# Rows of 264 for the second experts, normalised by ScalarE, with the expert chosen in the mixing, a shorter placing chain and mixing in five groups

## The chip, the cores and the metric

The kernel runs on one core of one Trainium2 chip. The metric is the time of one execution on the device in microseconds (us); for one core this is the core's own time from launch to end. Lower is better.

## The reference

A graph of 3125 nodes with 256 features and 50,000 edges goes through two attention layers, each followed by a feed-forward layer of experts. The change lies in the last two of the four parts. They compute, for x with one row per node:

```python
# L1_gnn, after the edges: agg, deg are sums over the edges of a node
msgs = jnp.where(deg[:, None, None] > 0, agg, V)
out = msgs.reshape(N, H * D) @ Wo + bo
x1 = out + node_features
x = x + (x1 - mu) / jnp.sqrt(var + 1e-05) * gamma + beta
# L1_ffn, on the layer norm of x: 32 experts, one per node, hidden size 64
xf = layernorm(x)
idx = jnp.argmax(xf @ router_w.T + router_b, axis=-1)
h = relu(jnp.einsum('nd,ndh->nh', xf, W1[idx]) + b1[idx])
x = x + relu(jnp.einsum('nh,nhd->nd', h, W2[idx]) + b2[idx])
```

## The kernel before

All arithmetic on features is in float32. Nodes are padded to 25 windows (WIN) of 128 rows; a window has one node per partition. Each part of the network is one or more blocks, and at the end of a block all engines meet at a barrier. The last three blocks are what the change touches.

**Mixing** (`mix_second`). The windows go through in groups, GROUPS_OF: five of 4 windows and one of 5. In round r VectorE does: `message(r + 2)` (sum of messages divided by its weight, or the node's own value where it has no edges; `val` is loaded from DRAM for that), the inverse standard deviation of the first norm, `apply_first(r)` (scale, gamma, residual into `k.comb[:, w, 0:D]`), the statistics of the second norm, `add_residual(r + 1)` (the product with Wo from PSUM plus `xin1_rows`, two windows per instruction), the statistics of the first norm of group r + 1, and at last `inverse(1, r)` and `second_shift(r)`. TensorE turns the messages (`turn`), multiplies by Wo (`multiply`, two windows per PSUM bank `ps_y`, three banks in a ring; the wait on `z_done` keeps a bank until `add_residual` has read it), and then, for group r, turns the normalised rows and makes the 32 logits of each node. ScalarE copies from PSUM to SBUF for each of these (`take_messages` in L2481, `xs` in L2507, logits in L2510), takes the square roots of the variances (`deviation`), and writes the normalised rows to `k.comb[:, w, D:2*D]` (L2502). Everything on an engine runs in the order of its code. In particular `deviation(1, r)` stands behind `take_messages(r + 2)` and behind the logits of group r - 1.

SyncE's queue loads `val` and `xin` two groups ahead. Its loop is: wait for `msg` of r, load `val` of r + 2, wait for `shift_ready` of r, load `xin` of r + 2. So the `val` of a group is issued behind the `xin` of the group before. After the loop it issues the weights of the second experts (L2385 to L2391).

**Placing** (`place`). VectorE adds the router's bias, takes the maximum, and makes `hot`, one of 32 for each of 25 x 128 nodes, by six instructions over 800 elements. TensorE multiplies `hot` by a matrix of ones (`ps_c`: nodes per window and expert) and by a triangle (`ps_b`: nodes before this one in its window); VectorE waits for both (`counted`, 2). It copies the counts, makes a running sum over the windows for each expert, rounds each expert's total up to whole tiles of 128, and from these makes each node's slot. GpSimd then scatters the 25 windows of `k.comb` to `sorted_rows` in DRAM, one indirect DMA per window (L2622). A row has COMB = 520 floats: x, the normalised x, and 8 copies of the node's number.

**Experts** (`feed_second`). 56 tiles of 128 sorted rows. For tile t, SyncE loads the tile (L2760) once tile t - 6 has been finished by VectorE (ring `rows`, IN = 6). TensorE's iteration t is: turn the rows of t (L2816), first product of t - 1 (L2827), turn the hidden rows of t - 2 (L2834), second product of t - 3 (L2839). ScalarE copies the turned rows (L2799) and applies the Relu (L2794). VectorE adds b1 (L2782), casts the node's number (L2772), and makes y (L2774). GpSimd scatters y to the output (L2749).

## Time and profile before

| | us |
|---|---|
| median of 3 runs | 1996.17 |
| lowest, highest | 1983.52, 2001.51 |
| the profiled execution | 1986.1 |
| its span, first to last instruction | 1984.4 |
| mixing, from the first instruction to the end of the block | 1699.8 to 1813.4 |
| placing, up to the slots | 1813.4 to 1836.5 |
| the scatter of the sorted rows, up to the next block | 1836.5 to 1874.2 |
| experts | 1874.2 to 1984.4 |

Times in the rows are microseconds from the span's start. The blocks are one after the other, so a block that is shorter moves all behind it. Of the engines, PE is TensorE's multiplying, PEld its loading of weights, DVE VectorE, ACT ScalarE, POOL GpSimd; SPq is SyncE's queue, and a DMA_DIRECT2D there is the issuing, not the transfer. What stands in brackets behind an instruction is the idle time of its engine before it and what ended it.

### The profile page before, as it was taken

The page shows a single profiled execution, that of the slowest core. Times are in us where ns is not written, and L with a number is a line of the kernel's source. Part 1 is how long each engine was busy: PE and PEld are TensorE (multiplying, and loading weights), DVE is VectorE, ACT ScalarE, POOL GpSimd, SP SyncE. Part 2 cuts the span into 40 slices and gives each one's busy share as a digit, 9 for nine tenths or more (in the row PEclk, how much of TensorE's full clock was granted, in tenths as well). Part 3 has the DMA queues.
Part 4 walks back from the last instruction along what each step waited for, and adds up shares of the span by engine and source line. Part 5 has one row for each costly group of instructions (what it writes and reads, how often), then busy time and mean ns, then how long its engine had stood idle before and what let it go on. Part 6 is the DMA issues. An engine that isn't in the chain of part 4 may idle for free. (4 is left out here: it accounts for less than half of the span.)

```text
span 1984.4 us, 29978 instructions
## 1 busy us (share of the span) xinstructions
PE 1396.1 (70%) x7038; PEld 974.9 (49%) x7038; DVE 1466.0 (74%) x3709; ACT 1114.5 (56%) x4299; POOL 1066.4 (54%) x1119
## 2 busy tenths in 40 slices
PE   5447656756666669998857787788877877674176
PEld 4334444444444457775534455555555554353154
DVE  5568778878878843366869999999999998776143
ACT  2247666676666643232533888888888887122033
POOL 2377777777776000003247777777777775100555
PEclk9667777777777759999977989988898888865599
DMA  5744444444443028001467767666777763225465
GB/s 123 196 128 125 138 124 125 125 136 125 124 137 85 1 75 299 1 1 48 159 213 232 203 199 207 200 197 200 200 202 203 201 199 123 64 65 120 167 197 138
DMA packets 141117, 287.90 MB, mean 145 GB/s; under 512 B 25507, under 2 KB 66977, under 8 KB 140821
## 3 DMA queue, kind: packets, MB, share of 16 engines
q0 software_dynamic: 58192, 175.85, 31.0%
q1 hardware_dynamic: 82758, 110.13, 18.9%
q8 instruction: 67, 1.10, 0.2%
q14 instruction: 100, 0.82, 0.1%
HBM read 241.17 MB, written 48.86 MB: 146 GB/s over the span
## 5 line engine op out<-in xcount | busy, mean ns | idle before, releaser
L773 POOL DMA_INDIRECT e_rows<-h_rows,src_col x416 | 433.0, 1041 | 127.0 <-issue 125.2
L1226 POOL DMA_INDIRECT e_rows<-kv_rows,src_col x320 | 309.0, 966 | 98.1 <-issue 60.6
L942 ACT ACTIVATE e_rows<-e_rows 128x32 f32<-128x32 f32 x1664 | 357.7, 305 | 0.8
L1011 PE MATMUL e_sum<-e_rows,e_of_dst 128*128 128x264 f32 x832 | 290.2, 501 | 77.8 <-DVE e_rows L870 71.3
L1481 ACT ACTIVATE e_rows<-e_rows 128x64 f32<-128x64 f32 x1168 | 292.8, 335 | 0.3
L1559 PE MATMUL e_query<-q,e_to_dst 128*128 x1248 | 215.4, 309 | 91.2 <-DVE e_rows L1294 70.5
L1011 PEld LDWEIGHTS e_sum<-e_rows,e_of_dst 128*128 128x128 f32 x832 | 194.0, 249 | 128.1 <-DVE e_rows L870 78.5
L1600 PE MATMUL e_sum<-e_rows,e_of_dst 128*128 128x260 f32 x640 | 202.9, 443 | 3.3 <-DVE acc L1382 2.9
L1559 PEld LDWEIGHTS e_query<-q,e_to_dst 128*128 128x128 bf16 x1248 | 124.6, 104 | 148.1 <-issue 105.9
L1382 DVE TENSOR_TENSOR acc<-acc,e_sum 128x260 f32 x299 | 125.7, 420 | 51.5 <-PE e_sum L1600 21.7
L1600 PEld LDWEIGHTS e_sum<-e_rows,e_of_dst 128*128 128x128 f32 x640 | 120.7, 212 | 30.9 <-DVE acc L1382 12.5
L2154 POOL TENSOR_TENSOR xb<-acc,bo 128x1280 f32<-128x1280 f32 x3 | 7.4, 2468 | 193.9 <-DMA beta<-in_L_gnn_beta 193.9
L1226 POOL DMA_INDIRECT x<-kv_rows,src_col x96 | 92.3, 961 | 33.8 <-issue 19.0
L1287 DVE TENSOR_TENSOR e_rows<-e_rows,e_relation 128x512 f32<-128x512 f32 x160 | 108.5, 678 | 1.4 <-DMA e_rows<-kv_rows,src_col 1.4
L1294 DVE TENSOR_TENSOR e_rows<-e_rows,e_query 128x512 f32<-128x512 f32 x160 | 108.0, 675 | 0.0
L1300 DVE TENSOR_REDUCE e_scores<-e_rows 128x8 f32<-128x512 f32 x160 | 107.7, 673 | 0.0
L880 DVE TENSOR_TENSOR acc<-acc,e_sum 128x264 f32 x208 | 86.7, 417 | 27.8 <-DVE e_bwd L799 14.0
L1552 PEld LDWEIGHTS e_relation<-rel,e_to_typ 64*128 64x128 bf16 x1248 | 52.7, 100 | 103.8 <-issue 71.5
L986 PE MATMUL e_turned<-ident,e_scores 128*128 128x128 f32 x26 | 12.1, 463 | 129.7 <-DVE e_scores L794 129.7
L1552 PE MATMUL e_relation<-rel,e_to_typ 64*128 64x64 bf16 x1248 | 78.2, 201 | 30.1 <-DVE e_to_dst L1278 12.7
L947 ACT ACTIVATE e_factor<-e_fall 8x1 f32<-8x1 f32 x26 | 5.3, 202 | 162.9 <-DVE e_fall L820 162.9
L1239 POOL TENSOR_TENSOR acc<-acc,e_taken 128x260 f32 x114 | 86.6, 760 | 18.6 <-DVE acc L1382 8.5
(420 smaller groups left out, 2993.4 us busy)
## 6 DMA issues: line engine op xcount, KB each, us to landing
sorted_rows<-zeros SPq DMA_DIRECT2D x1, 14560.0 KB
rows<-sorted_rows SPq DMA_DIRECT2D x56, 260.0 KB, 3.0
e_rel<-step_rel SPq DMA_DIRECT2D x26, 512.0 KB, 4.0
e_to_dst<-step_rel SPq DMA_DIRECT2D x52, 256.0 KB, 4.0
e_rows<-h_rows,src_col POOLq DMA_INDIRECT x416
e_to_typ<-step_typ SPq DMA_DIRECT2D x52, 128.0 KB
e_rows<-kv_rows,src_col POOLq DMA_INDIRECT x320, 3.7
kv_rows<-kv SPq DMA_DIRECT2D x5, 768.0 KB, 3.5
```

Of the source, the lines that this page charges most:

```text
L773: pool.indirect_dma_start(out=g[t // BATCH % R][:, t % BATCH, :], out_offset=None, in_=k.h_rows[:, :], in_offset=bass.IndirectOffsetOnAxis ...
L942: ins = act.activation(x, x, ACT.Copy, scale=row[:, D + h:D + h + 1])
L1011: pe.matmul(psm[t % NB], of_dst[q][:, s % GROUP, :], g[m % R][:, s, :], start=True, stop=True).then_inc(summed, 1)
L1226: pool.indirect_dma_start(out=rows_at(t, 1)[:, 0, :], out_offset=None, in_=k.kv_rows[:, :], in_offset=bass.IndirectOffsetOnAxis(ap=k.src_c ...
L1287: c.inc(v.tensor_tensor(keys, keys, ps_r[q % 2].unsqueeze(2).to_broadcast([P, QP, H, F]), ALU.add))
L1294: v.tensor_tensor(keys, keys, ps_q[q % 2][:, :, :], ALU.mult).then_inc(look_used, 1)
L1300: v.tensor_reduce(sc2[:, at, :], keys.rearrange("p s (h f) -> p s h f", h=H), AX_X, ALU.add).then_inc(scored, 1)
L1382: v.tensor_tensor(acc[:, w[t % 8], :], acc[:, w[t % 8], :], psm[t % NB], ALU.add).then_inc(added, 1)
L1481: ins = act.activation(x, x, ACT.Copy, scale=row[:, plo + h:plo + h + 1])
L1552: mm = pe.matmul(ps_r[q % 2][:, t, :], to_typ[h // 2 % 2][typ, s * P:(s + 1) * P], k.by_typ[typ, j, :], start=(j == 0), stop=(j == 2))
L1559: mm = pe.matmul(ps_q[q % 2][:, t, :], to_dst[h % 2][:, s * P:(s + 1) * P], k.by_dst[:, w[t], j, :], start=(j == 0), stop=(j == 2))
L1600: pe.matmul(psm[t % NB], of_dst[q % GROUPS][:, s % GROUP, :], rows_at(t, 1)[:, 0, plo:R1], start=True, stop=True).then_inc(summed, 1)
```

## The change

- `sorted_rows` and `k.comb` have COMB = D + 8 = 264 floats per row: x, the inverse deviation (RSTD), the shift (SHIFT1), and copies of the node's number (NODE).
- In the mixing ScalarE writes the normalised rows to a buffer `nx` that only the logits use. In the experts it makes them again, per tile, from x, RSTD and SHIFT1 (`norm`).
- The expert is chosen per group in the mixing (`choose`); `hot` is there when placing begins.
- GROUPS_OF has five groups, of 4, 6, 6, 6 and 3 windows.
- SyncE: `val` of r + 3 is issued before the wait for `shift_ready` of r; the weights of the experts are issued behind the `xin` of group 2, ahead of the `val` of group 4 and the `xin` of groups 3 and 4. The router's weights and Wo get a semaphore of their own, and VectorE waits for gamma and the bias later.
- Placing sums the counts of an expert straight from PSUM, finds the tiles from these, starts the running sum at the expert's first slot, and waits for `ps_b` only behind it.
- The memset under the hidden weights is dropped; the transpose of the hidden rows has 65 rows instead of 128.

```diff
-COMB = 2 * D + 8
+RSTD, SHIFT1, NODE = D, D + 1, D + 2
+COMB = D + 8
-GROUPS_OF = [(0, 4), (4, 8), (8, 12), (12, 16), (16, 20), (20, WIN)]
+GROUPS_OF = [(0, 4), (4, 10), (10, 16), (16, 22), (22, WIN)]
...
             load_val(0)
-            sp.dma_start(rw[:, :], a["L1_ffn_router_w"]).then_inc(loaded, 16)
+            sp.dma_start(rw[:, :], a["L1_ffn_router_w"]).then_inc(val_in[0], 16)
...
+            sp.wait_ge(msg, 1)
+            load_val(2)
             for r in range(NG - 2):
-                sp.wait_ge(msg, r + 1)
-                load_val(r + 2)
+                if r + 3 < NG:
+                    sp.wait_ge(msg, r + 2)
+                    load_val(r + 3)
                 sp.wait_ge(shift_ready, r + 1)
                 load_xin(r + 2)
...
+                if r:
+                    continue
+                for c in range(DC):
+                    sp.dma_start(k.w1_1[:, c, :, :], a["L1_ffn_W1"][:, c * P:(c + 1) * P, :].rearrange("e p h -> p e h")
...
+            def choose(r):
...
+                v.wait_ge(l_used, r + 1)
+                c.link(v.tensor_tensor(k.lg[:, lo:hi, :], k.lg[:, lo:hi, :],
+                                       k.rb[:, :].unsqueeze(1).to_broadcast(shape), ALU.add))
+                c.link(v.tensor_reduce(best[:, 0:n], k.lg[:, lo:hi, :], AX_X, ALU.max))
+                c.link(v.tensor_tensor(cell[:, 0:n, :], k.lg[:, lo:hi, :],
+                                       best[:, 0:n].unsqueeze(2).to_broadcast(shape), ALU.is_equal))
+                c.link(v.tensor_tensor(cell[:, 0:n, :], cell[:, 0:n, :], numbers, ALU.mult))
+                c.link(v.tensor_reduce(best[:, 0:n], cell[:, 0:n, :], AX_X, ALU.min))
+                c.link(v.tensor_tensor(k.hot[:, lo:hi, :], best[:, 0:n].unsqueeze(2).to_broadcast(shape), numbers,
+                                       ALU.is_equal))
...
             message(0)
-            v.wait_ge(loaded, all_loaded)
             v.wait_ge(rwt_t, 1)
...
             statistics(0, 0, lambda w: z[0][:, w, :])
+            v.wait_ge(loaded, all_loaded)
...
                 second_shift(r)
+                if r:
+                    choose(r - 1)
+            choose(NG - 1)
...
-                    act.activation(k.comb[:, w, D:2 * D], k.comb[:, w, 0:D], ACT.Identity, scale=rstd[:, 1, w:w + 1],
-                                   bias=shift[:, w:w + 1]).then_inc(normed, 1)
+                    act.activation(nx[r % 2][:, w - lo, :], k.comb[:, w, 0:D], ACT.Identity,
+                                   scale=k.comb[:, w, RSTD:RSTD + 1], bias=k.comb[:, w, SHIFT1:SHIFT1 + 1]
+                                   ).then_inc(normed, 1)
...
-            pe.wait_ge(loaded, all_loaded)
+            pe.wait_ge(val_in[0], 16 * (1 + FIRST_LOADS))
...
+            v.wait_ge(counted, 1)
             for half in range(2):
                 lo, hi = half * HW, min(WIN, (half + 1) * HW)
-                c.inc(v.tensor_copy(count[:, :, lo:hi], ps_c[half][:, 0:(hi - lo) * E1]
+                c.inc(v.tensor_reduce(half_sum[:, half, :], ps_c[half][:, 0:(hi - lo) * E1]
+                                      .rearrange("p (w e) -> p e w", e=E1), AX_X, ALU.add))
+            c.wait()
+            c.link(v.scalar_tensor_tensor(out=tiles_i[:, :], in0=half_sum[:, 0, :], scalar=float(P - 1),
+                                          in1=half_sum[:, 1, :], op0=ALU.add, op1=ALU.add))
+            c.link(v.tensor_single_scalar(tiles_i[:, :], tiles_i[:, :], 7, ALU.arith_shift_right))
+            c.link(v.tensor_copy(tiles[:, :], tiles_i[:, :]))
+            c.link(v.tensor_tensor_scan(until[:, :], k.ones[:, 0:E1], tiles[:, :], 0.0, ALU.mult, ALU.add))
+            c.link(v.tensor_tensor(tiles[:, :], until[:, :], tiles[:, :], ALU.subtract))
+            c.inc(v.tensor_scalar(count[:, :, 0], tiles[:, :], float(P), None, ALU.mult))
+            for half in range(2):
+                lo, hi = half * HW, min(WIN - 1, (half + 1) * HW)
+                c.inc(v.tensor_copy(count[:, :, lo + 1:hi + 1], ps_c[half][:, 0:(hi - lo) * E1]
...
-            c.link(v.tensor_copy(tiles_i[:, :], run[:, :, WIN - 1]))
-            c.link(v.tensor_single_scalar(tiles_i[:, :], tiles_i[:, :], P - 1, ALU.add))
...
-            c.link(v.tensor_tensor(run[:, :, :], run[:, :, :], count[:, :, :], ALU.subtract))
...
-            c.link(v.tensor_tensor(run[:, :, :], run[:, :, :], tiles[:, :].unsqueeze(2).to_broadcast([P, E1, WIN]),
-                                   ALU.add))
+            v.wait_ge(counted, 2)
...
+            def norm(t):
+                row = rows[t % IN]
+                act.wait_ge(rows_in[t % IN], 16 * (t // IN + 1))
+                wait(act, turned, t - HR + 1)
+                act.activation(nx[t % HR][:, :], row[:, 0:D], ACT.Identity, scale=row[:, RSTD:RSTD + 1],
+                               bias=row[:, SHIFT1:SHIFT1 + 1]).then_inc(nx_ready, 1)
+
+            norm(0)
+            norm(1)
             for t in range(SLOTS):
...
                 if t >= 2:
                     take_hidden(t - 2)
+                if t + 2 < SLOTS:
+                    norm(t + 2)
...
             def turn(t):
-                pe.wait_ge(rows_in[t % IN], 16 * (t // IN + 1))
+                pe.wait_ge(nx_ready, t + 1)
```

## Rows read from the trace of the kernel before

**Rows 1.** The page: the span.

```profile
span 1984.4 us, 29978 instructions
```

**Rows 2.** Windows: length, busy time by engine (instructions), TensorE clock, DMA share, GB/s.

```profile
1734.10:1751.60 17.50, 12.12 (x48) 9.67 (x48) 12.73 (x36) 5.60 (x15) 0.00 (x0) 0.71 0.20 60
...
1813.40:1836.50 23.10, 5.29 (x8) 2.50 (x8) 16.82 (x27) 0.00 (x0) 1.80 (x3) 0.57 0.02 4
1836.50:1874.20 37.70, 0.00 (x0) 0.00 (x0) 4.25 (x4) 0.00 (x0) 25.83 (x26) 0.50 0.46 177
...
1884.00:1984.40 100.40, 72.84 (x474) 54.02 (x472) 38.47 (x163) 34.00 (x105) 55.09 (x56) 0.97 0.60 166
```

**Rows 3.** Timeline of a round of the mixing: start, length, engine, line, what.

```profile
1734.07 0.16 DVE L2452 SCALAR_TENSOR_TENSOR shift<-mv,rstd 128x4 f32<-128x4 f32 x1
...
1734.66 0.51 SPq L2362 DMA_DIRECT2D val<-kv_rows  x1
...
1740.10 1.22 DVE L2408 TENSOR_TENSOR val<-val,nz 128x1024 f32<-128x1024 f32 x1 [4.03 <-DMA val<-kv_rows]
...
1743.79 2.08 PE L2536 MATMUL ps_y<-wo,mt 128*128 128x256 f32 x4
...
1748.66 1.97 PE L2536 MATMUL ps_y<-wo,mt 128*128 128x256 f32 x8 [0.97 <-DVE z L2435]
...
1751.54 0.16 DVE L2452 SCALAR_TENSOR_TENSOR shift<-mv,rstd 128x4 f32<-128x4 f32 x1
```

**Rows 4.** Timeline of the mixing: its start, and a group of five windows.

```profile
1711.33 0.23 DVE L2458 COPY rwt<-ps_l 128x64 f32<-128x64 f32 x1 [4.40 <-PE ps_l L2524]
...
1774.82 1.49 DVE L2408 TENSOR_TENSOR val<-val,nz 128x1280 f32<-128x1280 f32 x1 [3.88 <-DMA val<-kv_rows]
...
1804.46 2.56 ACT L2502 ACTIVATE comb<-comb,shift,rstd 128x256 f32<-128x256 f32 x5 [0.46 <-DVE shift L2452]
...
1812.80 0.29 ACT L2510 COPY logits<-ps_l 128x160 f32<-128x160 f32 x1 [1.17 <-PE ps_l L2555]
```

**Rows 5.** The experts' weights: timeline row, and DMA busy tenths in 40 slices, 1775 to 1836.

```profile
1787.55 6.17 SPq L2385 DMA_DIRECT2D w<-in_L_ffn_W  x2
...
DMA  0000000017999999999999999400000000000000
```

**Rows 6.** Timeline of the placing.

```profile
1813.40 0.20 DVE L2631 TENSOR_SCALAR place_number<-iota_row 128x32 f32<-128x32 f32 x1 [8.98 <-PEq L2302]
...
1819.41 0.99 DVE L2642 TENSOR_TENSOR place_hot<-place_best,place_number 128x800 f32<-128x800 f32 x1
...
1825.94 1.06 DVE L2647 COPY place_count<-ps_c 128x512 f32<-128x512 f32 x2 [5.54 <-PE ps_b L2686]
...
1836.30 0.18 DVE L2670 CAST slot_of<-place_slot 128x25 int32<-128x25 f32 x1
```

**Rows 7.** Indirect DMAs on GpSimd: ns min/median/max, first and last start.

```profile
L2622 POOL DMA_INDIRECT sorted_rows<-comb,slot_of x25: 967/970/2551, 1836.8 to 1868.9; - x25
...
L773 POOL DMA_INDIRECT e_rows<-h_rows,src_col x416: 942/947/2112, 75.2 to 633.6; - x139
```

**Rows 8.** Chain that ended last, in the experts: start, length, what.

```profile
1896.73 0.44 DVE y L2774
...
1897.18 2.93 DMA rows<-sorted_rows
...
1900.16 0.44 PE ps_t L2816 x2
...
1901.60 0.44 DVE y L2774
```

**Rows 9.** Experts: output scatters; landing of row loads; SyncE's queue, 1890 to 1970.

```profile
L2749 POOL DMA_INDIRECT out<-y,node x56: 982/982/997, 1884.5 to 1977.2; - x56
...
DMA to landing us min/median/max: 2.5/3.0/4.7
...
q1 hardware_dynamic: 6707, 12.42, 58.4%
```

More of the change, by code:

```diff
@@ L1923, in _ @@
         def _(pool):
-            pool.memset(zeros[:, 0:2 * D], 0.0).then_inc(zeros_ready, 1)
-            pool.memset(zeros[:, 2 * D:COMB], EMPTY).then_inc(zeros_ready, 1)
+            pool.memset(zeros[:, 0:NODE], 0.0).then_inc(zeros_ready, 1)
+            pool.memset(zeros[:, NODE:COMB], EMPTY).then_inc(zeros_ready, 1)
         @block.tensor
@@ L2325, in mix_second @@
         std = sb("std1", [P, 2, WIN])
-        rstd = sb("rstd1", [P, 2, WIN])
-        shift = sb("shift1", [P, WIN])
+        rstd = sb("rstd1", [P, WIN])
+        nx = [sb(f"nx{b}", [P, WMAX, D]) for b in range(2)]
+        number = sb("number", [P, E1])
+        best = sb("best", [P, WMAX])
+        cell = sb("chosen", [P, WMAX, E1])
         ps_m = [bank(f"ps4_m{i}") for i in range(2)]
@@ L2425, in inverse @@
                 v.wait_ge(std_ready, ln + 2 * r + which + 1 if not which or r == NG - 1 else ln + 2 * r + 3)
-                c.link(v.reciprocal(rstd[:, which, lo:hi], std[:, which, lo:hi]))
+                c.link(v.reciprocal(k.comb[:, lo:hi, RSTD] if which else rstd[:, lo:hi], std[:, which, lo:hi]))
             def add_residual(r):
@@ L2568, in _ @@
                     wait(pe, n_used, w - 1)
-                    turn(ps_n[w % 2], k.comb[:, w, D:2 * D]).then_inc(n_turned, 1)
+                    turn(ps_n[w % 2], nx[r % 2][:, w - lo, :]).then_inc(n_turned, 1)
                     if w > lo:
@@ L2585, in place @@
         before = sb("before", [P, P])
-        number = sb("number", [P, E1])
         cell = sb("cell", [P, WIN, E1])
-        best = sb("best", [P, WIN])
-        hot = sb("hot", [P, WIN, E1])
+        half_sum = sb("half_sum", [P, 2, E1])
         count = sb("count", [P, E1, WIN])
@@ L2608, in place @@
         block = ctx.enter_context(nc.Block())
-        marks = {}
         @block.gpsimd
@@ L2667, in _ @@
             c.wait()
-            c.link(v.tensor_tensor(cell[:, :, :], cell[:, :, :], hot[:, :, :], ALU.mult))
+            c.link(v.tensor_tensor(cell[:, :, :], cell[:, :, :], k.hot[:, :, :], ALU.mult))
             c.link(v.tensor_reduce(slot[:, :], cell[:, :, :], AX_X, ALU.add))
@@ L2680, in _ @@
         def _(pe):
-            pe.wait_ge(consts, 3)
-            pe.wait_ge(k.dve_steps, marks["hot"])
             for lhs, banks in ((k.ones, ps_c), (before, ps_b)):
+                if lhs is before:
+                    pe.wait_ge(consts, 3)
                 for half in range(2):
@@ L2686, in _ @@
                     mm = pe.matmul(banks[half][:, 0:(hi - lo) * E1], lhs[:, :],
-                                   hot[:, lo:hi, :].rearrange("p w e -> p (w e)"), start=True, stop=True)
+                                   k.hot[:, lo:hi, :].rearrange("p w e -> p (w e)"), start=True, stop=True)
                 mm.then_inc(counted, 1)
@@ L2706, in feed_second @@
         rows = [sb(f"rows5_{j}", [P, COMB]) for j in range(IN)]
+        nx = [sb(f"nx5_{j}", [P, D]) for j in range(HR)]
         xt = [sb(f"xt5_{j}", [P, DC, P]) for j in range(HR)]
-        hid = [sb(f"hid5_{j}", [P, P]) for j in range(HR)]
-        hid_t = [sb(f"hid5_t{j}", [P, P]) for j in range(HR)]
+        hid = [sb(f"hid5_{j}", [P, HID1 + 1]) for j in range(HR)]
+        hid_t = [sb(f"hid5_t{j}", [HID1 + 1, P]) for j in range(HR)]
         y = [sb(f"y5_{j}", [P, D]) for j in range(OUT)]
@@ L2742, in _ @@
         def _(pool):
-            for j in range(HR):
-                pool.memset(hid[j][:, HID1:HID1 + 1], 1.0).then_inc(hid_set, 1)
-                pool.memset(hid[j][:, HID1 + 1:P], 0.0).then_inc(hid_set, 1)
             for t in range(SLOTS):
@@ L2764, in _ @@
             load = experts(v, "dve_expert")
-            v.wait_ge(hid_set, 2 * HR)
+            for j in range(HR):
+                v.memset(hid[j][:, HID1:HID1 + 1], 1.0).then_inc(hid_ready, 1)
             v.wait_ge(k.w_in, 16 * (QKV_LOADS + DC + 3))
@@ L2771, in finish @@
                 wait(v, out_kept[j], 16 * (t // OUT))
-                v.tensor_copy(node[j][:, :], rows[t % IN][:, 2 * D:2 * D + 1]).then_inc(y_ready, 1)
+                v.tensor_copy(node[j][:, :], rows[t % IN][:, NODE:NODE + 1]).then_inc(y_ready, 1)
                 v.wait_ge(down, t + 1)
@@ L2812, in turn @@
             def turn(t):
-                pe.wait_ge(rows_in[t % IN], 16 * (t // IN + 1))
+                pe.wait_ge(nx_ready, t + 1)
                 wait(pe, xt_ready, t - 1)
                 for c in range(DC):
-                    mm = pe.transpose(ps_t[t % 2][:, c * P:(c + 1) * P], rows[t % IN][:, D + c * P:D + (c + 1) * P],
+                    mm = pe.transpose(ps_t[t % 2][:, c * P:(c + 1) * P], nx[t % HR][:, c * P:(c + 1) * P],
                                       k.ident[:, :])
@@ L2824, in raise_rows @@
                 pe.wait_ge(xt_ready, t + 1)
-                wait(pe, hid_ready, t - 1)
+                if t >= 2:
+                    pe.wait_ge(hid_ready, HR + t - 1)
                 for c in range(DC):
@@ L2895, in build @@
             k.b1_1 = sb(stage, "b1_1", [P, E1, HID1])
-            k.w2_1 = sb(stage, "w2_1", [P, E1, D])
+            k.w2_1 = sb(stage, "w2_1", [HID1 + 1, E1, D])
+            k.hot = sb(stage, "hot", [P, WIN, E1])
             k.rb = sb(stage, "rb", [P, E1])
```

68 lines of the change are left out of this document (28 added, 40 removed).

## The prediction

> **What bounds the kernel now.** I read the page for the span [rows 1], then the timeline and the windows of the last four stages, which run one behind the other; the change touches nothing before 1699.8 us except the store of zeros to `sorted_rows`, which is halved and lies under the first experts. What each stage waits for:
>
> In the mixing VectorE is the bound: busy 12.73 of 17.50 us in a round of four windows [rows 2]. The largest gap in the round is a wait for `val`: the load is issued right behind the shift of the round before, and VectorE stands 4.03 us for it [rows 3]. TensorE is nearly as busy (12.12 us), at a mean clock of 0.71 [rows 2].
>
> The placing is one serial chain of 23.1 us, with VectorE busy for 16.82 [rows 2]. The scatter is GpSimd's: 25 instructions in 37.7 us [rows 2, 7]. The experts are a loop of latencies, and no engine is full: TensorE is busy 72.84 of 100.4 us, GpSimd 55.09, ScalarE 34.00, the DMA engines 0.60 [rows 2]. The chain shows the loop: y of a tile, the load of the tile six further on, then turn, product, turn, product, and y of the tile three further on [rows 8].
>
> **Placing, removed and kept.** Before, from the block's start to the slots: 1836.48 - 1813.40 = 23.1 us [rows 6]. After: TensorE starts at once on the ones. Before, VectorE took its counts 5.54 us after `hot`, when both products were done [rows 6]; the ones are half of that, 2.8 us, and with the start I take 3.0. Then VectorE, by a fixed part and a part per element: 800 elements take 0.99 us [rows 6] and 1024 take 1.22 [rows 3], so about 1.04 ns per element and 0.16 us fixed, plus 0.03 between linked instructions. Two sums from PSUM of 512 and 288 elements 1.2; six instructions on 32 elements 6 x 0.23 = 1.4; two copies of 512 and 256 elements 1.1; the running sum over 800 elements, which is no plain instruction (I take twice one, 1.85); two additions from PSUM, also slower than plain (1.75); product and sum over 800 elements 2 x 1.02 = 2.05; the cast 0.2. Together 9.5, so 12.5 us and a gain of **10.6 us**. The product with the triangle is under the sums: it is done 2.8 us after the ones and wanted after 5.5. If a strided sum from PSUM cost double, the gain is 9.4; if the ones ran at 2.4 GHz, it is 12.
>
> **Choosing, moved into the mixing.** Six instructions per group; with n windows each has 32n elements: 0.33 us (n = 4), 0.39 (6), 0.29 (3). That is 2.0, 2.35 three times, and 1.75, together 10.8 us, where the 800 at once cost 6.1. VectorE's queue holds the next message and the first norm behind it. What of it counts depends on who is late in the rounds, so I follow them.
>
> **Mixing, round by round.** VectorE's round without the wait: 17.47 - 4.03 = 13.4 us for four windows [rows 3]. A fifth window makes each of the three message instructions 0.27 longer (1.22 to 1.49) [rows 3, 4]; residual, two statistics and two applications go by the same 256 elements each, so 0.8 + 0.3 + 0.8 + 0.8 = 2.7 per window. A round of six is 18.8 us, of which the message 5.9, `apply_first` 5.0, the statistics 2.5 each, the residual 1.9.
>
> Start: TensorE waited for the router's bias, the last small load, and VectorE 4.40 us for TensorE [rows 4]; now it needs only `val`, router weights and Wo, which are first in the queue. The gain is 4.1 us there.
>
> But TensorE and ScalarE change places with VectorE in the rounds of six. The ring has three banks of two windows. With groups of four, the first pair of the next messages finds a bank free and only the second waits for the residual, which the trace shows as 0.97 us at 1748.66 [rows 3]. With six, the group before fills all three banks: the first `multiply` of a group stands until `add_residual` has read its first pair. ScalarE's copies, and behind them `deviation`, and behind that VectorE's `inverse(1, r)`, wait for it. From that pair on, TensorE needs four products and four turns: a product takes 2.08 us at 1.2 GHz (1743.79) and 0.98 at 2.4 GHz (1748.66) [rows 3]; with 0.2 to 0.4 for a turn, 4.7 to 9 us. TensorE idles before it, as it did before 1743.79, where it ran at the low level, so I take 7.5 us. VectorE has 1.2 + 2.5 = 3.7 us of work in that time, so it stands some 4 us in each of rounds 0 and 1.
>
> With shifts at S(r): first statistics done at 1716.7; message 2 to 1722.7; application and statistics to 1728.1; first pair 1728.7; + 7.5, two deviations and inverse: S(0) = 1737.4, where before it was 1734.1 with fewer messages done. Round 1: message 1743.3, application and statistics 1751.0, pair 1751.7, S(1) = 1760.2. choose(0) to 1762.2. Round 2: `val` of group 4 is issued behind the weights. These took from 1787.55 to about 1813.7 (the busy slices end there, 1.525 us each) [rows 5], 26.2 us; issued at 1738.3 now, they end at 1764.5, and the `val` is there at about 1767. VectorE wants it at 1763.8: 3.2 us of waiting, with the same `val` wait as before in one round instead of four. Then message 1768.9, application and statistics 1776.6, residual and statistics 1781.0, S(2) = 1781.9. choose(1), then round 3: 1784.3, 1791.9, 1794.3, S(3) = 1795.1. In round 4 the deviation stands behind the logits of six windows. Five took 1812.80 - 1804.26 = 8.5 us behind their shift, 2.56 of it the norms [rows 4], so 1.7 per window at the low clock: 10.4 for six. S(4) = 1806.4. The logits of three windows take 5.3, the last choice 1.75, the barrier 0.3: 1813.8, where before placing began at 1813.40 [rows 6]. **Mixing: +0.4 us.** The gain of the earlier `val` and of one round less is eaten by the banks and the choice. Bounds: TensorE at 2.4 GHz throughout gives back 3 us in rounds 0 and 1 and 2.5 at the end, so -5; at 1.2 GHz throughout, and the weights' transfers slowing the `xin` of groups 3 and 4, +5.
>
> The Trainium skill (DMA: Bandwidth & Descriptors, "Queues, rings and completion order") says that each DMA engine consumes the descriptors of a ring in order. By it the `val` of group 4 stands behind all of the weights, as I took it; if transfers overtook each other, the 3.2 us would be gone. No row here has a small load behind the weights.
>
> **Scatter.** GpSimd's time does not go by row length: 970 ns for rows of 2080 bytes, 947 for the gathers of 264 floats at L773 [rows 7]. 25 times 1.27 us stay. Only the last landing is shorter, by half of its 0.8 us of transfer (8 packets per engine at 0.111 us, below): **-0.4 us**.
>
> **Experts.** The loop before: y to load 0.45, load L, landed to next y 1901.60 - 1900.11 = 1.49 [rows 8], so 1.94 + L for three tiles. The pace is (1977.2 - 1884.5) / 55 = 1.685 us per tile [rows 9], 5.06 for three, so L = 3.12 on average; landings are 2.5 at least, 3.0 in the median [rows 9]. A packet of 2080 bytes holds its engine for 0.584 x 16 x 80 / 6707 = 0.111 us [rows 9]; a load has 8 per engine, 0.89 us, and 1.61 of the least landing are not transfer. With half the bytes: if only the load's own packets shrink, L = 3.12 - 0.45 = 2.67; if all above 1.61 halves, waiting included, 2.37. I take the middle, 2.52, since the output's writes stay. Against it stands the norm. It runs two tiles ahead in ScalarE's code, but the load of tile t is started by y of t - 6, and norm, turn, products and y of t - 3 follow: it is on the same loop of three tiles. It costs 0.51 (2.56 for five) [rows 4] and 0.05 for the signal. Net -0.60 + 0.56 = -0.04 per loop, and 56/3 = 18.7 loops: **-0.8 us**; the first tile, one norm later and landed 0.45 sooner, is +0.1. Bounds: -0.75 + 0.51 gives -4.5; no shorter landing and a norm of 0.6 gives +11. ScalarE has the room: 34.00 + 56 x 0.56 = 65 of 100 us, and GpSimd's 1.28 per tile is under 1.67.
>
> The same page ("Anatomy of one DMA") puts some 2.0 us of a DMA down to setup and completion, whatever its size. By that L would be 2.0 + 1.12/2 = 2.56 and the sum would stay; by the trace the fixed part is 1.61.
>
> The rest (memset of the hidden weights, 65 instead of 128 rows in one transpose, halved zeros) is 0: GpSimd was idle beside it, matmul time goes by columns, and a shorter store of zeros can only gain; I put it at nothing because no instruction of the last stages waits for it.
>
> **Sum.** +0.4 - 10.6 - 0.4 - 0.8 + 0.1 = -11.3 us. The profiled execution, 1986.1 with a span of 1984.4 [rows 1], goes to 1974.8. It was 10 us below the median of the runs; the same difference off 1996.17 gives 1984.9.
>
> **Rivals.**
> - Faster by over 1%: it takes 20 us. With TensorE at 2.4 GHz in the mixing (-5) and everything of a landing above 1.61 halved (-4.5), the sum is -10.6 - 0.4 - 5 - 4.4 = -20.4, 1975.8. For it: TensorE stays busier once VectorE waits less. Against it: it idles for 6 us and more ahead of each residual.
> - The shorter rows do not shorten the landing, and the norm is added: +11 in the experts, sum 0.3, 1996. For it: most of 2.5 is no transfer. Against it: landings of 2.5 to 4.7 in a queue that is busy 0.60 of the time must hold some waiting for transfers.
> - Slower: TensorE falls to 1.2 GHz in the experts. It idles each time ScalarE stands for a load, and then both it and the copy are late. Its part of the loop, 1.41 us, doubles: 18.7 x 1.4 = +26, sum +15, 2011. It decides from about half of the loops on. Against it: clock 0.97 now at the same pace [rows 2].
>
> **Numbers.** Forecast (-17 to -5 us) 0.6, faster rival 0.2, no shorter landing 0.15, clock 0.05. Over 1% faster 0.2, within 1% 0.76, over 1% slower 0.04 (1% is about what a measurement of this kernel can tell from no change). The likeliest case's own range is 1979 to 1991; with the faster rival and the runs' own spread of 18 us below, and most of the case without shorter landing above, 1966 to 1996.
>
> **What would show it.** Placing: slots 12.5 us behind the block's start. Mixing: TensorE's `multiply` of groups 2 and 3 released by z, two waits of VectorE of about 4 us for the deviation, one of about 3 us for `val`, the block's end within 5 us of 1813.8. Experts: landing median 2.3 to 2.6, pace 1.67 per tile, norms released by loads. It is wrong if the pace is under 1.6 or over 1.8, or if the mixing ends before 1808.

## The result, and the profile after

| | before | after |
|---|---|---|
| median, us | 1993.92 | 2009.18 |
| runs | 10 | 10 |
| lowest, highest | 1983.52, 2001.51 | 1999.85, 2017.50 |
| ratio to before | | 1.0083 [1.0065, 1.0101] |
| span of the profiled execution | 1984.4 | 1998.1 |

The changed kernel is slower, by 0.8%, where I had forecast 11 us less. The 95% interval of the ratio stands in brackets. By stage, in the profiled executions (us):

| stage | before | after | difference | forecast |
|---|---|---|---|---|
| all ahead of the mixing | 1699.8 | 1695.1 | -4.7 | 0 |
| mixing | 113.6 | 114.7 | +1.1 | +0.4 |
| placing, up to the slots | 23.1 | 12.2 | -10.9 | -10.6 |
| scatter, up to the next block | 37.7 | 37.4 | -0.3 | -0.4 |
| experts | 110.2 | 138.7 | +28.5 | -0.7 |

Three of the four stages came out within 1 us of what was worked out. For the difference ahead of the mixing I found no cause in the change; the runs' own spread is 18 us. All that is lost lies in the experts. These are the windows of after, by the stages and then within the experts; the columns are the length, then busy time and instructions of PE, PEld, DVE, ACT and POOL, then TensorE's granted clock, the DMA share and GB/s.

```profile
1695.10:1809.80 114.70, 68.03 (x303) 56.13 (x303) 87.26 (x240) 35.37 (x91) 0.65 (x2) 0.66 0.42 108
1809.80:1822.00 12.20, 4.70 (x8) 2.17 (x8) 9.61 (x19) 0.00 (x0) 0.60 (x3) 0.64 0.00 0
1822.00:1859.40 37.40, 0.00 (x0) 0.00 (x0) 4.27 (x4) 0.00 (x0) 25.89 (x25) 0.50 0.25 90
1862.00:1868.00 6.00, 5.62 (x24) 4.83 (x25) 0.73 (x4) 4.25 (x12) 0.00 (x0) 0.50 0.24 71
...
1880.00:1990.00 110.00, 109.02 (x432) 93.94 (x432) 35.00 (x148) 52.61 (x142) 48.59 (x50) 0.50 0.29 83
```

The last row answers to the last of [rows 2]. There the clock was 0.97 (2.4 GHz nearly all the time) and TensorE busy 72.84 of 100.4 us. Here it is 0.50 (1.2 GHz) from the first tile to the last, and TensorE is busy 109.02 of 110 us: it has become the bound. It did not fall to the low level for want of work; it was full and stayed there. Before, the stage began at the low level too, and then the clock rose. This is the window of before ahead of the last of [rows 2], with a mean clock of 0.53 in it and 0.97 behind it:

```profile
1874.00:1884.00 10.00, 6.88 (x32) 5.91 (x33) 1.16 (x5) 2.42 (x7) 0.43 (x6) 0.53 0.50 160
```

The chain of after that ended last, in the same stage: start, length, what. Where [rows 8] went through y, a load and the turns, this one goes through TensorE alone, tile after tile.

```profile
1901.92 0.43 PE ps_t L2847 x2
1902.34 0.75 PE ps_u L2859 x4
1903.09 0.21 PE ps_h L2866
1903.31 0.86 PE ps_y L2871 x2
1904.16 0.43 PE ps_t L2847 x2
```

A tile is 0.43 + 0.75 + 0.21 + 0.86 = 2.25 us of TensorE. The output's scatters say the same, from first to last of 56, with the landing of the row loads under them:

```profile
L2768 POOL DMA_INDIRECT out<-y,node x56: 982/985/997, 1869.5 to 1990.9; - x56
...
rows<-sorted_rows SPq DMA_DIRECT2D x56, 132.0 KB, 2.1
```

(1990.9 - 1869.5) / 55 = 2.207 us per tile, against 1.685 in [rows 9]. The loads land in 2.1 us in the median, where it was 3.0 and I had 2.52: the shorter rows do what they were taken to do, and it is of no use, since the loop that they shorten no longer sets the pace.

### The profile page after: what moved, and what is told of

Read it like the earlier page. It is cut to its first block and busy times, and to the rows that moved or that the text cites. A ratio compares the mean times of both kernels' runs of the same rounds, so it can differ in the third digit from the quotient of the medians.

```text
span 1998.1 us, 30095 instructions
## 1 busy us (share of the span) xinstructions
PE 1427.1 (71%) x7038; PEld 1015.7 (51%) x7038; DVE 1464.9 (73%) x3726; ACT 1140.2 (57%) x4352; POOL 1057.6 (53%) x1112
## 5 line engine op out<-in xcount | busy, mean ns | idle before, releaser
L1601 PEld LDWEIGHTS e_sum<-e_rows,e_of_dst 128*128 128x128 f32 x640 | 120.2, 211 | 30.0 <-DVE acc L1383 12.2
L2768 POOL DMA_INDIRECT out<-y,node x56 | 55.1, 985 | 81.3 <-DVE y L2794 78.9
```

The lines of the kernel that those rows point to most:

```text
L1601: pe.matmul(psm[t % NB], of_dst[q % GROUPS][:, s % GROUP, :], rows_at(t, 1)[:, 0, plo:R1], start=True, stop=True).then_inc(summed, 1)
```

## The experiments

**Which theories.** The clock is the symptom, so the question is what keeps it low. The change touches TensorE's work in the experts in three ways. The hidden rows are transposed over 65 columns and multiplied over 65 rows, where before both were padded to 128. (The line of the product is not in the diff: it became shorter because both its operands did.) The turns wait for a norm on ScalarE, where they waited for a load. And the loads are shorter. I held the 65 rows for the cause (theory A; ROWS in the expectations). The rival was the new start of the loop: behind the norms TensorE's work comes in another rhythm, the clock never gets its first rise, and at 1.2 GHz the loop holds itself there (theory B; NORM).

The chips of these runs are slower ahead of the mixing (it begins at 1896.2 us in experiment 1, at 1695.1 in after; the kernel before takes 2193 to 2216 us on them). So medians are given as ratios to before on the same chip, and stages in us. Experiments 1 to 3 and the first kernel of experiment 4 shared one chip, all but the repeat of experiment 1, so the low and the high clock below are seen on the same chip.

**1. The changed kernel with all of the padding back.** Hidden rows, their transposes and the weights behind them have 128 columns or rows again, zeros from the 66th on. With the wider weights their memset and a wait for it come back, as the kernel before had them. Nothing else differs.

```diff
+                sp.wait_ge(numbered, 2)
...
+            pool.memset(k.w2_1[HID1:P, :, :], 0.0).then_inc(numbered, 1)
...
-        hid = [sb(f"hid5_{j}", [P, HID1 + 1]) for j in range(HR)]
-        hid_t = [sb(f"hid5_t{j}", [HID1 + 1, P]) for j in range(HR)]
+        hid = [sb(f"hid5_{j}", [P, P]) for j in range(HR)]
+        hid_t = [sb(f"hid5_t{j}", [P, P]) for j in range(HR)]
...
-                v.memset(hid[j][:, HID1:HID1 + 1], 1.0).then_inc(hid_ready, 1)
+                v.memset(hid[j][:, HID1:HID1 + 1], 1.0)
+                v.memset(hid[j][:, HID1 + 1:P], 0.0).then_inc(hid_ready, 1)
...
-                pe.transpose(ps_h[t % 2][0:HID1 + 1, 0:P], hid[t % HR][:, :], k.ident[:, :]).then_inc(hid_turned, 1)
+                pe.transpose(ps_h[t % 2][:, 0:P], hid[t % HR][:, :], k.ident[:, :]).then_inc(hid_turned, 1)
...
-            k.w2_1 = sb(stage, "w2_1", [HID1 + 1, E1, D])
+            k.w2_1 = sb(stage, "w2_1", [P, E1, D])
```

> The changed kernel with the hidden rows of the experts' stage turned and multiplied over 128 rows again, as before (second weights padded to 128 rows with zeros); all else of the change stays. In the changed kernel TensorE runs at 1.2 GHz through the whole stage (granted clock 0.50 from 1862 to 1988, pace 2.21 us per tile), though it never waits. Theory ROWS (operands of 65 rows and columns are why the clock isn't raised): clock 1.00 some 7 us behind the stage's start, pace 1.6 to 1.7 us per tile, stage about 105 us instead of 139, time about 1975 us against 2009 of the changed kernel. Rival NORM (ScalarE's norm in front of each turn, or shorter rows, changes the rhythm of TensorE so that the clock stays low): clock 0.50 as in the changed kernel, about 2009 us.

Measured: 2182.91 against 2192.74 us, ratio 0.9951 [0.9927, 0.9976]. The experts take 114.5 us (2060.5 to 2175.0). Its windows:

```profile
2062.00:2070.00 8.00, 6.51 (x32) 5.73 (x33) 1.16 (x5) 5.26 (x13) 0.00 (x0) 0.56 0.31 88
2070.00:2078.00 8.00, 6.32 (x42) 4.45 (x40) 3.55 (x15) 4.41 (x13) 4.72 (x5) 1.00 0.43 125
...
2086.00:2166.00 80.00, 64.74 (x388) 48.86 (x387) 31.18 (x134) 44.16 (x127) 43.32 (x45) 0.94 0.37 101
```

The norm, the short rows and the six-tile ring are all there, and the clock rises as it did before. The gain in the stage is 24 us, less than the 34 expected. The whole kernel is now faster than before by 0.5%, some 11 us. It also ran as the base of the kernels of experiment 5, on their chip.

> The same kernel as after128 (changed kernel, hidden rows over 128 rows again), beside the next three on one chip. All theories: 0.5% faster than the kernel before, clock 1.00 for most of the experts' stage, pace about 1.75 us per tile.

Measured: ratio 0.9949 [0.9920, 0.9978], experts 110.7 us (2087.3 to 2198.0). It repeats.

**2. The kernel before with 65 rows.** The other direction: neither the norm nor the short rows are there.

```diff
-        hid = [sb(f"hid5_{j}", [P, P]) for j in range(HR)]
-        hid_t = [sb(f"hid5_t{j}", [P, P]) for j in range(HR)]
+        hid = [sb(f"hid5_{j}", [P, HID1 + 1]) for j in range(HR)]
+        hid_t = [sb(f"hid5_t{j}", [HID1 + 1, P]) for j in range(HR)]
...
-                pool.memset(hid[j][:, HID1 + 1:P], 0.0).then_inc(hid_set, 1)
...
-                pe.transpose(ps_h[t % 2][:, 0:P], hid[t % HR][:, :], k.ident[:, :]).then_inc(hid_turned, 1)
+                pe.transpose(ps_h[t % 2][0:HID1 + 1, 0:P], hid[t % HR][:, :], k.ident[:, :]).then_inc(hid_turned, 1)
...
-                pe.matmul(ps_y[t % 2][:, 0:D], hid_t[t % HR][:, :], k.w2_1[:, e[t], :], start=True, stop=True
+                pe.matmul(ps_y[t % 2][:, 0:D], hid_t[t % HR][:, :], k.w2_1[0:HID1 + 1, e[t], :], start=True, stop=True
```

> The kernel before with that one part of the change: hidden rows turned to 65 rows and multiplied over 65 rows; nothing else. ROWS: the clock stays at 0.50 in the experts' stage, pace 2.2 us per tile instead of 1.69, so 25 to 30 us slower than before, about 2020 us. NORM: no difference to the kernel before, 1994 us, clock 1.00 in the stage.

Measured: ratio 1.0133 [1.0084, 1.0183], +29 us. The experts take 138.6 us (2075.5 to 2214.1).

```profile
2078.00:2086.00 8.00, 7.65 (x33) 6.60 (x34) 1.44 (x7) 2.62 (x8) 0.32 (x1) 0.50 0.45 151
2086.00:2094.00 8.00, 8.00 (x34) 6.70 (x32) 2.56 (x10) 2.10 (x8) 3.64 (x4) 0.50 0.58 171
2094.00:2206.00 112.00, 111.01 (x441) 96.08 (x440) 35.76 (x151) 31.41 (x98) 49.64 (x51) 0.50 0.49 136
```

The whole loss of the stage, 28 us, comes with the 65 rows alone, in a kernel that has nothing else of the change. Experiment 1 has the norms and the short rows and a high clock. So theory B falls as the cause.

**3. A dense start.** Can the clock be lifted once, and does it then stay? Five products of 128 x 512 stand in front of the first turn of the changed kernel.

```diff
+            for _ in range(5):
+                pe.matmul(ps_y[1][:, :], k.ident[:, :], k.x[:, 0:2, :].rearrange("p w d -> p (w d)"),
+                          start=True, stop=True)
```

> The changed kernel with five extra products of 128 x 512 (their result is not used) in front of the first turn of the experts' stage, so that TensorE is busy 128 rows wide without a gap for about 8 us. If the loop can hold 2.4 GHz once it is there: clock 1.00 behind the burst to the end, pace 1.6 to 1.7, stage about 139 + 6 - 32 = 113 us. If the loop itself does not keep the clock: it rises in the burst and falls again within some us, pace 2.2, stage about 145 us. ROWS expects the second, NORM leaves both open.

Measured: 2199.53 us in one run, where the changed kernel itself wasn't run on this chip; the experts take 138.9 us (2058.9 to 2197.8). Its windows:

```profile
2062.00:2064.00 2.00, 2.00 (x3) 0.68 (x3) 0.00 (x0) 0.17 (x1) 0.00 (x0) 0.50 0.53 156
2064.00:2066.00 2.00, 2.00 (x7) 0.83 (x6) 0.00 (x0) 0.00 (x0) 0.00 (x0) 0.98 0.00 0
...
2072.00:2074.00 2.00, 1.11 (x8) 0.98 (x9) 0.35 (x1) 1.09 (x4) 1.55 (x2) 1.00 0.60 156
2074.00:2076.00 2.00, 1.84 (x9) 1.39 (x9) 0.71 (x3) 1.71 (x5) 0.74 (x2) 0.58 0.40 123
2076.00:2078.00 2.00, 2.00 (x10) 1.71 (x9) 0.71 (x3) 1.20 (x3) 0.67 (x1) 0.50 0.29 84
...
2084.00:2190.00 106.00, 104.70 (x417) 90.63 (x415) 33.94 (x143) 50.72 (x136) 46.85 (x48) 0.50 0.29 82
```

The dense products lift the clock to 2.4 GHz, it holds for some ten microseconds of the loop, and falls at about 2074, behind a stretch with TensorE busy 1.11 of 2.00 us. From then on TensorE is full and the clock does not come back for the remaining 116 us. The kernel of experiment 1 passes a stretch as thin (busy 1.00 of 2.00 us, 2136 to 2138) with its clock at 1.00. So a missed first rise is not what is wrong: a lift is lost again, and full work of this kind does not win it back. The five products did not make the stage 6 us longer, as I had expected: 138.9 us against 138.7.

**4. Which of the two operations.** First the transpose alone over 128 in the changed kernel (`hid` [P, P] with zeros, the product still over 65).

> The changed kernel with only the transpose of the hidden rows over 128 columns again (LDWEIGHTS of 128 columns); the second product stays over 65 rows. ROWS, if the transposes carry it: clock 1.00, stage about 105 us. ROWS, if the second product, which is 40% of TensorE's time in the loop (0.86 of 2.25 us), carries it: clock 0.50, stage 139 us. NORM: 0.50.

Measured, in one run: clock 0.50 throughout, 138.1 us of experts. The transpose is not what decides.

```profile
2080.00:2190.00 110.00, 108.97 (x435) 94.13 (x433) 35.46 (x149) 52.89 (x142) 48.69 (x50) 0.50 0.30 83
```

Then the product alone over 128 (weights and their memset as in experiment 1, `hid_t` [P, P] set to zero once at the stage's start, the transpose still over 65), and the mirror of it: the kernel before with only the product over 65, which is one line.

```diff
-                pe.matmul(ps_y[t % 2][:, 0:D], hid_t[t % HR][:, :], k.w2_1[:, e[t], :], start=True, stop=True
+                pe.matmul(ps_y[t % 2][:, 0:D], hid_t[t % HR][0:HID1 + 1, :], k.w2_1[0:HID1 + 1, e[t], :], start=True, stop=True
```

> The kernel after with the hidden values transposed as there (65 rows, hidden tile of 65 columns), but the second product over 128 rows, with 63 rows of zeros on both sides. The run with only the transpose over 128 kept the clock at 0.50 through the experts. Theory (it is the second product over 65 rows that keeps the clock low): the clock goes to 1.00 within the first 15 us of the experts and the stage takes 108 to 116 us, as in the kernel after with both over 128 rows (114.5 and 110.7). Rival (either of the two 65-row operations is enough, both have to go): clock 0.50 to the end and 138 to 140 us.

> The kernel before with one line changed: the second product over 65 of the 128 rows; the transpose stays over 128 and all waits stay. Theory (the product is enough): clock 0.50 for the whole stage, 138 to 140 us of experts, some 28 us above before on this chip. Rival (the transpose counts, or both together): clock 1.00 from about 10 us after the first product and 108 to 112 us of experts.

Measured, windows of the changed kernel with the product over 128:

```profile
2088.00:2096.00 8.00, 3.63 (x17) 3.10 (x18) 0.43 (x5) 3.82 (x10) 0.00 (x0) 0.50 0.36 101
2096.00:2104.00 8.00, 6.55 (x38) 5.23 (x37) 2.98 (x13) 4.31 (x13) 2.97 (x3) 0.84 0.30 83
2104.00:2190.00 86.00, 71.66 (x436) 52.36 (x434) 33.80 (x144) 49.94 (x147) 47.71 (x49) 0.96 0.40 110
```

and of the kernel before with the product over 65:

```profile
2092.00:2100.00 8.00, 8.00 (x35) 7.14 (x35) 2.15 (x11) 2.60 (x8) 1.99 (x2) 0.50 0.33 86
2100.00:2212.00 112.00, 112.00 (x453) 97.76 (x451) 35.49 (x151) 32.48 (x100) 49.12 (x50) 0.50 0.51 143
```

The experts take 113.8 us (2089.5 to 2203.3) in the first and 138.3 us (2086.4 to 2224.7) in the second. The one product decides by itself: in the changed kernel, putting it back over 128 is enough for the high clock, and in the kernel before, putting it over 65 is enough for the low one. The whole kernels took 2205.16 and 2226.41 us in one run each, before 2216.05 beside them. The 28 runs of before beside experiment 5 spread over 26 us, so the stage is what counts here.

The 65 rows do not make an instruction slower or faster. These are groups of the stage in the kernel of experiment 2, all at the low level; then two in the kernel with the product over 128, where most ran at the high level (busy us, mean ns of one); and last the product over 128 rows at the low level, in experiment 1 from 2094 to 2099 (ns min/median/max).

```profile
L2838 PE MATMUL ps_y<-w,hid_t 65*128 x102 | 54.2, 635 | 0.0
L2826 PEld LDWEIGHTS ps_u<-w,xt 128*128 128x128 f32 x206 | 50.4, 334 | 0.0
...
L2838 PEld LDWEIGHTS ps_y<-w,hid_t 65*128 65x128 f32 x103 | 28.5, 338 | 0.0
```

```profile
L2863 PEld LDWEIGHTS ps_u<-w,xt 128*128 128x128 f32 x219 | 30.7, 201 | 7.5 <-issue 3.0
L2875 PE MATMUL ps_y<-w,hid_t 128*128 x112 | 36.2, 407 | 0.0
```

```profile
L2874 PE MATMUL ps_y<-w,hid_t x5: 634/634/634, 2094.1 to 2098.6; 128*128 x5
```

The product takes 635 ns over 65 rows and 634 over 128, and a weight load of 65 x 128 takes 338 ns where one of 128 x 128 takes 334. The Trainium skill (TensorE: Matmul & The Clock Gate, "Step-by-step: what each phase is for") says that a load's time scales with the columns and not with the rows, and the trace agrees: with 65 columns instead of 128, the load of the hidden rows takes 231 ns in experiment 2 and 337 in the kernel before with only the product over 65. But here the clock itself hangs on the rows.

**5. What bounds the repaired kernel.** With the padding back, three things could be had: the ring (ScalarE's norms waited 27.6 us for loads between 2080 and 2165 in experiment 1), the deviations in the rounds of six windows, and the `val` behind the weights. First a ring of 12 tiles, loaded in pairs:

```diff
-        rows = [sb(f"rows5_{j}", [P, COMB]) for j in range(IN)]
+        rows = [sb(f"rows5_{j}", [P, 2, COMB]) for j in range(IN)]
...
-            for t in range(SLOTS):
-                wait(sp, y_ready, 2 * (t - IN + 1))
-                sp.dma_start(rows[t % IN][:, :], k.sorted_rows[t * P:(t + 1) * P, :]).then_inc(rows_in[t % IN], 16)
+            for q in range(SLOTS // 2):
+                wait(sp, y_ready, 4 * (q - IN + 1))
+                sp.dma_start(rows[q % IN][:, :, :], k.sorted_rows[2 * q * P:2 * (q + 1) * P, :]
+                             .rearrange("(j p) d -> p j d", p=P)).then_inc(rows_in[q % IN], 16)
...
```

> after128 with the tiles loaded in pairs into a ring of six pairs, twelve tiles instead of six (rows are half as long, so the memory is that of the kernel before); all else as after128. Theory LOOP (the tiles' pace is a loop of latencies: y, load, norm, turn, products, y, and the norm stands on it): with the load off the loop the pace falls from 1.75 to what the engines need, ScalarE 1.23 us per tile plus signals and GpSimd 1.28, so 1.3 to 1.4, 20 to 25 us less than after128. Rival ENGINES (ScalarE or the clock limits the pace): 1.7 stays, no gain.

Measured: ratio 0.9960 [0.9929, 0.9990], which can't be told from its base (0.9949), though the stage of the profiled execution is 107.1 us (2076.5 to 2183.6) against 110.7. The 20 to 25 us that theory LOOP expected did not come; the rival's "no gain" is nearer. The loads are off the path all the same: these are groups of the stage, 2097 to 2170.

```profile
L2824 ACT ACTIVATE nx<-rows 128x256 f32<-128x256 f32 x44 | 26.1, 593 | 0.0
L2863 PEld LDWEIGHTS ps_u<-w,xt 128*128 128x128 f32 x177 | 23.2, 191 | 12.0 <-issue 12.0
```

The norms stand 0.0 us for loads, and the stage is 3.6 us shorter, no more than single executions differ by. So the waits for loads, 27.6 us in experiment 1, were hardly what set the pace. What is left is TensorE, busy 76.60 of 90 us from 2080 to 2170, and gaps that the profile calls issue, 12.0 us ahead of the first product's weight loads; from 2120 to 2160 the chain has a piece of 0.66 to 0.69 us of it every 6.2 to 7.0 us. What they are I can't say; no run took them apart. Then the grouping: six groups as before with the weights still issued early, and at last six groups with the weights issued last, together with the ring of 12.

```diff
-GROUPS_OF = [(0, 4), (4, 10), (10, 16), (16, 22), (22, WIN)]
+GROUPS_OF = [(0, 4), (4, 8), (8, 12), (12, 16), (16, 20), (20, WIN)]
```
```diff
-                if r:
+                if r < NG - 3:
                     continue
```

> after128 with the mixing in six groups of four and five windows, as before; all else of the change stays. If the banks of the ring are what a group of six waits for (theory BANKS): no wait of VectorE for the deviation of 3 to 4 us in the rounds, and TensorE's multiply waits under 1 us for z. But the weights now stand in front of the val of group 4 by a round of 15 us instead of 23, so VectorE waits about 11 us for it instead of 4.5: mixing 114 to 119 us against 114.7, time within 0.3% of after128. Rival: groups of six cost nothing, and six groups only add a round's fixed 2.7 us and a longer wait: mixing over 120 us.

> ring12 with six groups in the mixing and the experts' weights issued behind the last xin, as before, so that no val stands behind them. BANKS and LOOP together: VectorE's waits in the mixing shrink to under 1 us per round, mixing about 107 us instead of 114.7, experts as in ring12: 28 to 33 us less than after128, about 2% under the kernel before.

| | mixing and placing, us | waits for deviation | wait for `val` | ratio to before |
|---|---|---|---|---|
| experiment 1 again: five groups, weights early | 128.6 | 13.3 | 4.5 | 0.9949 [0.9920, 0.9978] |
| six groups, weights early | 134.4 | 2.2 | 13.1 | 0.9965 [0.9941, 0.9990] |
| six groups, weights last, ring of 12 | 121.0 | 2.2 | 0 | 0.9908 [0.9878, 0.9937] |

The second column goes from the first instruction of the mixing to the slots, in the profiled execution; in that of before it was 113.6 + 23.1 = 136.7 us. The other kernels with five groups and early weights (after, experiment 1, the ring of 12) have 126.7 to 126.9, so one execution is good to 2 us here. VectorE's waits, first in before and then in the three kernels in the order of the table: us in total, times, the longest.

```profile
DVE val L2408 <- DMA val<-kv_rows: 14.0, 4, 4.0
```

```profile
DVE comb L2436 <- ACT std L2519: 13.3, 5, 4.6
DVE val L2418 <- DMA val<-kv_rows: 4.5, 1, 4.5
```

```profile
DVE val L2418 <- DMA val<-kv_rows: 13.1, 1, 13.1
DVE logits L2473 <- ACT logits L2545: 7.0, 1, 7.0
...
DVE comb L2436 <- ACT std L2519: 2.2, 6, 0.4
```

```profile
DVE comb L2436 <- ACT std L2519: 2.2, 6, 0.4
```

With six groups the waits for deviations are gone, as theory BANKS has it, but the mixing itself took 122.1 us and not the 114 to 119 expected: what is saved there is lost at the one `val` behind the weights, 13.1 us, and at the last group's logits, 7.0 us where five groups have 3.2. The last kernel beats both: 2190.68 us where before takes 2211.05 and the base 2198.46. That is 8 us under the base and not the 28 to 33 expected, since the 20 to 25 of theory LOOP are missing; the mixing gives 6 to 8 of it. The early issue of the weights was no gain in six groups: without it mixing and placing are 13.4 us shorter, the 13.1 us at one `val`. Whether five groups are a gain is not shown, since none of these kernels has five groups with the weights last. By the base's own waits, leaving out its 4.5 us for `val` would bring it to some 124 us (an estimate: 128.6 - 4.5), or 122 off the 126.7 of its other executions, against 121.0 with six. What the order of the `val` loads is worth shows in the last kernel: before, the waits for them came to 14.0 us in four rounds, and there no round waits for one. No kernel has this order alone.

## Why the prediction was wrong

**The step that failed** is the one that stood last and was put at nothing: "65 instead of 128 rows in one transpose ... 0 ... matmul time goes by columns". There were two faults in it. I named only the transpose, which indeed costs nothing (experiment 4), and overlooked, in the description of the change too, that the second product behind it also ran over 65 rows. And the rule I used is a rule for the length of one instruction at a given clock. It holds (635 ns over 65 rows, 634 over 128), and yet that product over 65 of 128 rows, 0.86 of the 2.25 us of a tile in the chain, keeps the clock of the whole stage at 1.2 GHz. It costs 24 to 28 us: 138.7 against 110.7 and 114.5 in the changed kernel, 138.6 and 138.3 against 110.2 in the kernel before.

**The rival that came true** is the third, "TensorE falls to 1.2 GHz in the experts", with a chance of 0.05. Its price was near, by luck: +26 forecast, +28.5 measured, 2011 forecast, 2009.18 measured. Its cause was another. I let it hang on TensorE idling more, and argued it away with the clock of 0.97 at the same pace. The trace shows TensorE idle for 1 of 110 us. The argument compared paces and not what was multiplied, so it spoke about a different mechanism from the one at work. And the price is the result of another sum: not 18.7 loops, each longer by TensorE's 1.4 us, but 56 tiles at TensorE's full 2.25 us, 126 us where the stage had 110.2, and its start and end on top.

**Placing, -10.6**: measured -10.9, and its steps hold. This is its timeline in after.

```profile
1809.76 3.00 PE L2707 MATMUL ps_c<-hot,ones 128*128 128x512 f32 x4 [2.63 <-PEq L2303]
...
1812.80 1.05 DVE L2665 TENSOR_REDUCE place_half_sum<-ps_c 128x32 f32<-128x512 f32 x2 [2.11 <-PE ps_c L2707]
...
1816.16 1.82 DVE L2680 TENSOR_TENSOR_SCAN place_run<-place_fresh,place_count 128x800 f32<-128x800 f32 x1
1818.02 1.71 DVE L2686 TENSOR_TENSOR place_cell<-place_run,ps_b 128x512 f32<-128x512 f32 x2
...
1821.81 0.18 DVE L2691 CAST slot_of<-place_slot 128x25 int32<-128x25 f32 x1
```

Forecast, with the measured value in brackets: the ones are done 3.0 us after the start (3.0), the running sum takes 1.85 (1.82), the additions from PSUM take 1.75 (1.71). A strided sum from PSUM did not cost double (1.05 for both, against 1.2). Slots stand 12.2 us behind the block's start, forecast 12.5.

**Mixing, +0.4**: measured +1.1. The banks of the rounds of six are there as worked out, as is the `val` behind the weights; a timeline of TensorE and VectorE in after:

```profile
1724.98 1.62 PE L2569 MATMUL ps_y<-wo,mt 128*128 128x256 f32 x3 [5.35 <-DVE z L2444]
1731.91 0.18 DVE L2435 RECIPROCAL comb<-std 128x4 f32<-128x4 f32 x1 [3.24 <-ACT std L2518]
1754.67 0.19 DVE L2435 RECIPROCAL comb<-std 128x6 f32<-128x6 f32 x1 [4.34 <-ACT std L2518]
1763.05 0.96 DVE L2417 TENSOR_TENSOR val<-val,nz 128x768 f32<-128x768 f32 x1 [4.51 <-DMA val<-kv_rows]
```

VectorE stands 3.24 and 4.34 us in the first two rounds (some 4 forecast) and 4.51 for the `val` of group 4 (3.2 forecast). With groups of four, all else equal, TensorE's waits for z fall from 20.4 us to 2.5 and VectorE's for deviations from 13.3 to 2.2 (experiment 5), which bears the banks out. The start gained less than the 4.1 us forecast: VectorE copies the turned router weights 11.5 us into the block before and 8.6 in after, 2.9 us. One part of the rest is that `val`, the router's weights and Wo now raise one semaphore, so that the first message waits 3.86 us, for Wo, where it waited 2.41 for `val`. The other long wait for a deviation, 4.08 us at 1801.73, is that of round 4, whose deviation stands behind the logits of six windows; it was in the working, though not among the signs that I named. The rule of the Trainium skill about rings (DMA: Bandwidth & Descriptors, "Queues, rings and completion order") now has its row: the load of 384 KB issued behind the weights lands in 14.0 us (14.0 to 14.5 in the runs with five groups), the larger one of 640 KB in 5.5 us where the weights come last and in 14.0 where they come early, both with six groups. The trace agrees with it.

**Scatter, -0.4**: -0.3.

**Experts, -0.7**: never seen in the changed kernel, since TensorE set the pace, but seen with the padding back: 110.7 and 114.5 us against 110.2, so +0.5 and +4.3. Both terms were off in size. The landing went from 3.0 to 2.1 us in the median of after (2.3 to 2.6 was the sign; 2.52 forecast for the loop's 3.12), and the norm takes 0.60 instead of 0.51. The least landing is 1.9 us, so the fixed part is under the 2.0 us that the prediction quotes from the Trainium skill (DMA: Bandwidth & Descriptors, "Anatomy of one DMA", a section on DMAs that GpSimd issues, while these are SyncE's). That the two cancel is no more than the spread of 4 us allows to be said. And with the loads off the norms' path altogether the stage is 3.6 us shorter, not 20 (experiment 5): that a loop through the load sets the pace of the repaired kernel is not shown. The sum of all, -11.3 us, agrees with the repaired kernel: 0.9951 and 0.9949 of 2193 and 2211 us are -10.7 and -11.3 us, with intervals from -5 to -16 and from -5 to -18. The sum was right, within that, for a kernel that differs from this one in the padding.

**The range** ended at 1996, and the clock rival, at 2011, lay outside it with a chance of 0.05. Both rested on that rival being argued away from one row, with no bound taken for an operation whose shape changed and whose effect on the clock no row that I had read could show.

## What to carry to other kernels

Padding of an operand may not be waste to be tidied up: here it held TensorE's clock up. Count, for each TensorE operation whose rows, columns or rhythm an edit changes, what the stage costs at 1.2 GHz, and keep that as the bound of the range. When a stage slows down after an edit, read the granted clock beside the busy time first: TensorE full at 0.50 says that its work got slower, not more. And test a bundle of edits by putting back its smallest part; here that one part turned +0.8% into -0.5%, and undoing two others together with a longer ring gave another 0.4%.

## What the runs showed of the hardware that I had not expected

- TensorE busy for 109.02 of 110.00 us, 111.01 of 112.00 and 112.00 of 112.00 us in three kernels, at a granted clock of 0.50 all along. Only the rows of one product, 65 or 128, decide in these kernels between that and 0.94 to 0.97 behind the first microseconds of the stage. The Trainium skill (TensorE: Matmul & The Clock Gate, "What's actually happening") has the clock go by how busy the engine has been. The busy time of the profile can't be what is meant: by it the clock would have risen here, and the measurement decides. Why the rows count no run shows, and other numbers of rows than 65 and 128 were not tried. Not every product over few rows does it: in before, from 1150 to 1550 us, 762 products of L1552 over 64 rows (bf16, 46.7 of TensorE's 318.55 us busy) run among others over 128 rows at a mean clock of 0.90. Here the product over 65 rows is 0.86 of 2.25 us and float32; which of these differences matters is open. The 63 rows of the padding hold zeros on both sides of the product, and they make the difference nevertheless.
- With the product over 128 rows the clock has dips too, but it comes back. In windows of experiment 1 one dip lies between 2092 and 2100. In it TensorE is as full as in after and takes the same 2.25 us for a tile (0.21, 0.85, 0.43 and 0.75 us in the chain); after some 7 us the clock is at 1.00 again, where with 65 rows it stayed down for 110 us and more:

```profile
2084.00:2092.00 8.00, 6.20 (x36) 4.10 (x36) 3.24 (x13) 3.99 (x13) 4.43 (x6) 1.00 0.46 134
2092.00:2100.00 8.00, 7.44 (x31) 6.35 (x32) 2.01 (x9) 3.86 (x13) 2.69 (x3) 0.57 0.20 54
...
2096.00:2098.00 2.00, 2.00 (x10) 1.71 (x9) 0.71 (x3) 0.66 (x3) 0.98 (x1) 0.50 0.27 69
...
2100.00:2102.00 2.00, 2.00 (x17) 1.65 (x15) 1.07 (x6) 1.00 (x3) 0.98 (x1) 1.00 0.44 133
```

- So each form of this stage has one pace to which it returns: with 128 rows about 1.7 us per tile, the clock high and TensorE idle a fifth to a quarter of the time, also after a dip; with 65 rows 2.2 us, the clock low and TensorE full, also after a lift (experiment 3).
